# The folded down weight's way out of its PSUM banks, moved from VectorE to ScalarE

## What is computed

```
xn = layernorm(x)
s  = Wo(phi(q) * cumsum(phi(k) * v)) + bo          # phi = elu + 1, q, k, v = linear(xn)
h  = silu(fwht(xn * SU_ug) @ W_gate.T ...) * (fwht(xn * SU_ug) @ W_up.T ...)
z  = fwht(h * SU_dp) @ W_down.T * Wscale_dp        # h has 2048 features, z 512
out = x + s * silu(z)
```

## Time and profile before

| | |
|---|---|
| median of 3 runs | 1351.02 us (1350.25 to 1351.17) |
| the profiled execution | 1350.48 us |
| its span | 1348.7 us |
| granted TensorE clock | 0.996 of full |
| TensorE matmuls busy | 1309.1 us, 97% |
| VectorE busy | 1010.2 us, 75% |
| ScalarE busy | 459.4 us, 34% |

### The profile page before, as it was taken

How to read it: one execution, slowest core, us unless ns; L and a number is a source line. 1 busy time by engine, 2 the same in 40 slices (tenths; PEclk the granted TensorE clock), 3 DMA queues, 4 the chain that set the end, 5 groups by cost and what they waited for, 6 DMA issues and landing times. The chain is left out here.

```text
span 1348.7 us, 16107 instructions
## 1 busy us (share of the span) xinstructions
PE 1309.1 (97%) x6100; PEld 598.3 (44%) x6100; DVE 1010.2 (75%) x1618; ACT 459.4 (34%) x683; POOL 51.4 (4%) x85
## 2 busy tenths in 40 slices
PE   3998999999999999999999999999999999999998
PEld 2543444444454444444444444444444444444443
DVE  5689999987847998778735998778743998787333
ACT  4744564462123443332112433332111443332000
POOL 0022210011100000000000000000000000000000
PEclk8999999999999999999999999999999999999999
DMA  9414655467664323325244332334253423333230
GB/s 375 191 63 164 203 214 198 166 237 268 204 226 162 128 94 126 125 98 183 94 156 154 127 126 99 120 125 160 101 169 113 169 102 125 113 106 126 94 125 32
DMA packets 48125, 200.96 MB, mean 149 GB/s; under 512 B 5296, under 2 KB 5552, under 8 KB 32560
## 3 DMA queue, kind: packets, MB, share of 16 engines
q1 hardware_dynamic: 41424, 176.87, 36.8%
q0 software_dynamic: 6624, 23.07, 4.8%
HBM read 154.83 MB, written 45.09 MB: 148 GB/s over the span
## 5 line engine op out<-in xcount | busy, mean ns | idle before, releaser
L1415 PE MATMUL bank<-xops,ring 128*128 128x512 f16 x2772 | 601.1, 379 | 3.2 <-DVE work L886 2.9
L1415 PEld LDWEIGHTS bank<-xops,ring 128*128 128x128 f16 x2772 | 269.7, 98 | 334.1 <-DVE work L886 11.2
L886 DVE TENSOR_TENSOR work<-bank,work 128x512 f32<-128x512 f32 x462 | 305.1, 684 | 92.4 <-PE bank L1415 85.6
L1481 PE MATMUL bank<-ring,h_all 128*128 128x512 f16 x1536 | 334.0, 379 | 0.8 <-DVE gate_g L1150 0.8
L1322 PE MATMUL bank<-xops,ring 128*128 128x512 f16 x1056 | 238.4, 383 | 12.4 <-DVE ring L984 7.4
L1481 PEld LDWEIGHTS bank<-ring,h_all 128*128 128x128 f16 x1536 | 150.3, 98 | 180.8 <-DVE gate_g L1150 1.3
L1322 PEld LDWEIGHTS bank<-xops,ring 128*128 128x128 f16 x1056 | 103.5, 99 | 149.2 <-issue 23.4
L675 ACT ACTIVATE h_all<-work 128x512 f16<-128x512 f32 x128 | 80.1, 627 | 210.4 <-DVE work L925 210.4
L1150 DVE TENSOR_TENSOR gate_g<-bank,row 128x512 f32<-128x512 f32 x32 | 21.4, 688 | 106.7 <-PE bank L1481 106.2
L934 DVE TENSOR_TENSOR h_all<-work,h_all 128x512 f16<-128x512 f32 x128 | 87.1, 683 | 0.4
L725 ACT ACTIVATE gate_g<-gate_g 128x512 f32<-128x512 f32 x32 | 19.9, 630 | 191.9 <-DVE gate_g L1150 191.9
(11 more groups left out here) (145 smaller groups left out, 876.3 us busy)
## 6 DMA issues: line engine op xcount, KB each, us to landing
ring<-scr_g SPq DMA_DIRECT2D x66, 1024.0 KB, 4.8
ring<-scr_d SPq DMA_DIRECT2D x32, 1024.0 KB, 4.8
scr_g<-ring SPq DMA_DIRECT2D x22, 512.0 KB, 3.7
scr_g<-ring POOLq DMA_DIRECT2D x22, 512.0 KB, 3.5
h_all<-in_ug_t SPq DMA_DIRECT2D x8, 1024.0 KB, 20.4
ring<-scr_f POOLq DMA_DIRECT2D x16, 512.0 KB, 4.5
x_res<-in_x SPq DMA_DIRECT2D x32, 256.0 KB, 3.6
out<-x_res SPq DMA_DIRECT2D x32, 256.0 KB, 6.8
```

The lines of the kernel that those rows point to most:

```text
L886: dve.tensor_tensor(tile(g, to), bank[product][:, :], tile(g, other), ALU.add).then_inc(summed, 1)
L1415: mm = pe.matmul(bank[n][:, :], weight_of(slot, s, b, kk), xops[:, kk, xs, c, :], start=(a == 0), stop=(a == 5))
L1481: mm = pe.matmul(bank[D_BANK[t]][:, :], at[:, s, cols], w[:, :, ws, :], start=(a == 0 and b == 0 and n == 0), stop=(a == KB - 1 and b == K ...
```

## The change

The take of the folded down weight leaves VectorE and goes to ScalarE. In place of one VectorE product over 128x512, ScalarE makes four copies of 128x128, each with one column of `coef_e` as its per-partition scale. They stand in ScalarE's program at the same places (8, 10, 12, 14) of each piece. Since ScalarE now reads `coef_e`, it waits for a new semaphore that `scale_down` counts, and `scale_down` waits, from the second piece on, until the four takes before it are done.

```diff
+        d_coef_made = sem("d_coef_made")
@@ ScalarE
+            def take_down(e, j):
+                act.wait_ge(d_coef_made, e + 1)
+                act.wait_ge(d_folded, 4 * e + j + 1)
+                for k in range(KB):
+                    last = act.activation(fly_down[:, j, k, :], bank[DOWN_FOLD_BANK[j % 2]][:, P * k:P * k + P],
+                                          ACT.Copy, scale=coef_e[:, KB * j + k:KB * j + k + 1])
+                last.then_inc(d_scaled, 1)
@@ ScalarE, first_group
+                    if at in TAKE_DOWN_AT:
+                        take_down(e, TAKE_DOWN_AT.index(at))
                     if at == DOWN_HIGH_AT:
                         down_high(e)
@@ VectorE, scale_down
+                if e:
+                    dve.wait_ge(d_scaled, 4 * e)
                 prep.after(dve.tensor_scalar(coef_e[:, :], coef_down[:, :], s_d[:, at], None, ALU.mult))
...
-            def take_down(e, j):
-                dve.wait_ge(d_folded, 4 * e + j + 1)
-                src = bank[DOWN_FOLD_BANK[j % 2]][:, :].rearrange("p (k n) -> p k n", k=KB)
-                dve.tensor_tensor(fly_down[:, j, :, :], src,
-                                  coef_e[:, KB * j:KB * j + KB].unsqueeze(2).to_broadcast([P, KB, P]),
-                                  ALU.mult).then_inc(d_scaled, 1)
+                dve.sem_inc(d_coef_made, 1)
@@ VectorE, first_weights
-                    elif at in TAKE_DOWN_AT:
-                        take_down(e, TAKE_DOWN_AT.index(at))
```

## The result

| | before | after |
|---|---|---|
| median | 1350.25 us (11 runs, 1349.00 to 1352.08) | 1353.83 us (11 runs, 1353.06 to 1354.97) |
| span of the profiled execution | 1348.7 us | 1353.2 us |
| VectorE busy | 1010.2 us | 1001.2 us |
| ScalarE busy | 459.4 us | 475.3 us |

The changed kernel is slower: the ratio is 1.0026, with a 95% interval of 1.0017 to 1.0035. Of 1350.25 us that is 3.5 us.

What follows compares the result with a forecast made beforehand. The prediction saw a loop through ScalarE's high part and VectorE's butterflies to TensorE's first folds as the bound. First folds 2.59 us plus load 0.87 made 3.46 us on 1351.02, so 1354.5 us, range 1351.0 to 1356.2.

Steps and rivals of the forecast that it cites:

- What bounds the kernel: Loop from TensorE's tile over ScalarE's high part, VectorE's low part and 22 us of VectorE to the first fold.
- What it takes away: Sixteen VectorE products, 2.4 us a piece; all turns into longer waiting unless ScalarE's high part comes earlier, by 0.30 us at most.
- What it adds: Four ScalarE copies per take, 0.36 us each, pushing what stands behind them by 1.04 us; bounds 0.36 to 1.48 us.
- The first folds: TensorE's first folds of down pieces 1, 2 and 3 come later by 1.04, 0.74 and 0.81 us, 2.59 in all.
- The load behind piece 3: Store and made-weight load after piece 3 come 1.04 us later; TensorE waits 0.87 us, from below 0.
- The sum: Whole kernel: 2.59 + 0.87 = 3.46 us added to the median 1351.02, giving 1354.5 us, 0.26% slower.
- The cheap case: Rival: copies are cheap or the tail absorbs them; 1353.6 us without the last term, 1351.7 with cheapest copies; chance 0.22.
- The gain: Rival: VectorE's freed time reaches the first folds and their 1.12 us of waits vanish; 1349.9 or 1349.1 us; chance 0.08.
- The late takes: Rival: ScalarE's in-order queue makes takes late, delaying the fourth fold and tiles, 1 us per piece; 1358.5 us; chance 0.08.
- What I said would show it: Profile signs: VectorE busy down 11 us, ScalarE up some 23, L631 wait 2 us or more, first-fold waits some 3.7.

Runs made afterwards that it cites:

- second trace: The changed kernel, unaltered, run and profiled once more against the kernel before: 1354.25 us, ratio 1.0028 (the second comparison).
- x2: Against the kernel before, only the fourth take of each piece moved to ScalarE, the other three left on VectorE: 1355.47 us, ratio 1.0032.
- x3: The changed kernel with each copy of the fourth take cut into four of 32 columns: 1364.2 us, ratio 1.0096; run again 1366.0 us, ratio 1.0111.
- x7: The changed kernel with only the fourth take of piece 3 given back to VectorE: 1353.86 us, ratio 1.0023 to the kernel before.

## Why the prediction was right

**What bounds the kernel.** Shown. The loop from gate tile over high part, low part and VectorE's butterflies to the first fold is what the change hit. The two moves of the fourth take and the kernels with earlier high parts bear it out from both sides.

**What it takes away.** Right: VectorE's 2.4 us per piece became waiting time. Its wait for the high part rose by 1.00 us at piece 1 and not by more, because it waits elsewhere first: it is idle for 2.11 us ahead of its up tile at 190.66, where it was idle for 0.19 before. TensorE ends that tile, 47, at about 190.1; the last 0.5 us the trace doesn't explain. This wait I had not seen. With the 0.24 us behind `scale_down` the three make 1.00 + 1.92 + 0.24 = 3.16 us more of idle time, which is the 2.4 us set free and the 0.76 us by which the piece took longer. This changes nothing of the sum. Nor does a slip: the new wait in `scale_down` is for takes six tiles back, from place 14 to place 4, and not eight, and the trace of the changed kernel shows no idle time ahead of `coef_e`.

**What it adds.** A copy of 128 columns was put at 0.36 us and measured 0.367. Four push what is behind them by 1.00 us (193.95 to 194.95), where I had 1.04. The estimate by the prices of the Trainium skill (ScalarE: Activation LUTs, What ACT_TABLE_LOAD costs), 1.17 us for four, is not borne out: it is 0.17 too much. The rule of the Trainium skill (ScalarE: Activation LUTs, Rules for kernel authors) to keep multiplications on VectorE fits the one take of four that stands on the loop, and not the other twelve of the sixteen, nor any of them once the high part is early (1348.16 us with the takes on ScalarE, 1348.50 with them on VectorE).

**The first folds.** 2.59 us were predicted and 2.63 measured, piece by piece 1.04, 0.74, 0.81 against 1.04, 0.76, 0.83.

**The load behind piece 3.** The mechanism was right and the size off: 0.87 us predicted. By the rows under "The store and the load behind the last piece" it cost 23.83 - 23.31 = 0.52 us, and 0.31 in the second trace of the same kernel. The store and the start of the load were late by 1.04 us, as predicted. Two things made less of it, as this row of the changed kernel shows for the first, the load (its time to landing, 8.7 before):

```profile
DMA to landing us min/median/max: 8.5/8.5/8.5
```

In the second trace it was 8.3. The other is that I read the slack from TensorE's weight load, 0.17 us, and the product itself had some 0.4 us (313.55 less 313.16).

**The sum.** 3.46 us predicted, 3.5 measured. The time predicted, 1354.5 us, is 0.7 over the measured 1353.83 only because it starts from the median of three runs, 1351.02, and that of eleven is 1350.25. The terms that the trace shows make 2.63 + 0.52 = 3.15 us, and in the second trace 2.60 + 0.31 = 2.91. The rest, 0.4 us of the 3.5 and 0.9 of the 3.8 that the second comparison gives, is within the intervals and has no cause shown. A part may be the wait at L1157, 1.1 and 1.3 us in the two traces against 0.8 before, and a part the lower clock at piece 0, below. That the total came out closer than its last term is luck.

**The rivals.** The cheap case is out by the measured 1.00 us of four copies. The gain is out as the change was made. The earlier place takes the three waits away, but it does so with or without VectorE's freed time, so not by the way of that rival. The late takes are out: the second take of piece 1 ended at 180.35 us and the fourth fold stood at 186.60.

**What I said would show it.** VectorE's busy time fell by 9 us (11 said) and ScalarE's rose by 15.9, where I had said 23: I had added up means, and the profile's page counts overlapping copies once.

## What to carry to other kernels

Before work is moved from a busy engine to an idle one, find what the busy engine waits for around that work: where it already waits for the idle one, the move only lengthens the wait, and what comes to stand between the two counts by as much as it pushes what is behind it. Here 12 of 16 moved takes were free and 4 cost everything. What decided was the place in an in-order queue: setting a producer ahead of an instruction that waits for TensorE brought both kernels to 0.15% under the kernel before (from 1354.25 to 1348.16 us for the changed one), with no work removed.

## What was unexpected of the hardware

A wait of TensorE can cost more than its length. The twelve traces hold 20 first folds with a wait of 1.2 to 1.8 us, and behind all of them the next 24 matmuls took 5.34 us. They hold 16 with a wait of 2.9 to 3.4 us, and behind 8 of these the same matmuls took 6.6 or 7.0 us, with a mean granted clock of 0.72 to 0.81 over the 6 or 7 us, behind the other 8 they took 5.34 us. In these 16 the longer waits had the stretch behind them more often: all 5 of 3.25 to 3.36 us, 3 of the 8 of 3.03 to 3.19, none of the 3 of 2.95 to 2.98. The length doesn't decide alone, since 3.04 us stands on both sides. What decides was not tried. Such a stretch reaches the kernel pair itself, at the first fold of piece 0, which the change doesn't touch. In the trace of before TensorE waited 2.98 us there and the next tiles ran at full clock; in the trace of the changed kernel:

```profile
110.82 1.12 PE L1372 MATMUL bank<-ring,hada 128*128 128x512 f32 x2 [3.36 <-DVE ring L1102]
111.79 7.03 PE L1327 MATMUL bank<-xops,ring 128*128 128x512 f16 x24
```

That is 1.7 us, and since this execution had come to the fold 0.6 us sooner, 1.1 of the 4.5 by which the two spans differ. It is no work of the change: the first of its takes comes at 120.9 us, and the traces of x2, x3 and x7, which have the change in part or with more copies, don't have the stretch there. Two single traces would have made the change about a quarter worse than it is; the spacing from fold to fold kept it apart. Both traces of the changed kernel have it, and both are of the slowest execution of their comparison (1354.97 of 11, 1354.69 of 7), so its median may hold some of it too; how much is not shown.

The other is small: behind the last instruction of `scale_down` VectorE was idle for 0.24 us at pieces 1 to 3, where before the next instruction followed without a wait. All that the change adds at this place is the count of the new semaphore, as an instruction of its own. Counting it on the last instruction instead was not tried.
